# Attention and expert layer on one core: one burst of values for a pair of heads, three banks for transposed probabilities, first keys from ScalarE's queue

## The reference, cut to what matters

```
q = (layernorm(x, g_in) @ Wq) -> 16 heads of 64, * 64**-0.5
k, v = split(layernorm(x, g_in) @ Wkv)              # one head, 64 each
k, v = concat([null_k, k]), concat([null_v, v])     # a null key and value in front
sim = q @ k.T + concat([null_bias, attn_bias])      # 512 x 513 for each head
sim = where(causal or masked, -max, sim)
out = softmax(sim) @ v                              # heads side by side: 512 x 1024
x = x + layernorm(out @ Wo, g_out)
x = x + moe(x)
```

## Time and profile before

| what | value |
|---|---|
| runs | 1820.24, 1817.81, 1814.46 us; median 1817.81 |
| the profiled execution | 1821.24 us, span 1819.5 us |
| TensorE matmul busy | 1644.0 us, 90% of the span |
| TensorE weight load busy | 1369.8 us, 75% |
| VectorE busy | 982.2 us, 54% |
| ScalarE busy | 712.3 us, 39% |
| GpSimd busy | 735.4 us, 40% |
| mean granted TensorE clock | 0.959 of 2.4 GHz |

### The profile page before, as it was taken

One profiled execution on the slowest core, in us unless ns is written; L12 is line 12 of the kernel. 1 busy time (PEld: TensorE's weight loads), 2 busy tenths in 40 slices (PEclk: granted clock), 3 DMA queues, 4 the chain that ended last, 5 costly groups with the idle time before them and its releaser, 6 DMA issues. The chain is left out here.

```text
span 1819.5 us, 36436 instructions
## 1 busy us (share of the span) xinstructions
PE 1644.0 (90%) x10388; PEld 1369.8 (75%) x10389; DVE 982.2 (54%) x2454; ACT 712.3 (39%) x1819; POOL 735.4 (40%) x1204
## 2 busy tenths in 40 slices
PE   6899986999999999996888998869999999879998
PEld 4677766887888888885777776758778788668886
DVE  5434535776777776775544554634334344355555
ACT  3222325776777676772222121103333333311221
POOL 1000234676676676673545551132222222143223
PEclk9989997999999999997999997979999999889999
DMA  6565657776676676766343342043466533244423
GB/s 217 197 209 201 226 205 214 205 219 194 186 221 199 190 224 186 209 181 191 115 136 129 128 151 91 0 174 104 173 225 228 181 104 105 91 145 130 142 92 116
DMA packets 172582, 301.79 MB, mean 166 GB/s; under 512 B 16691, under 2 KB 64355, under 8 KB 170421
## 3 DMA queue, kind: packets, MB, share of 16 engines
q1 hardware_dynamic: 142324, 235.21, 40.2%
q0 software_dynamic: 11280, 35.99, 6.8%
q10 hardware_dynamic: 18864, 29.38, 4.7%
HBM read 187.26 MB, written 113.26 MB: 165 GB/s over the span
## 5 line engine op out<-in xcount | busy, mean ns | idle before, releaser
L737 POOL TENSOR_SCALAR probs<-probs,rsums 128x512 f32<-128x512 f32 (+3 forms) x512 | 265.1, 536 | 199.3 <-DVE rsums L773 199.2
L765 DVE CUSTOM_DVE_ANT_0 scores<-psum,resident 128x514 f32<-128x514 f32 (+3 forms) x512 | 242.8, 484 | 155.3 <-PE psum L880 135.5
L838 ACT ACTIVATE probs<-scores,lowest 128x514 f32<-128x514 f32 (+3 forms) x512 | 284.2, 558 | 33.4 <-DVE lowest L765 32.2
L892 PE MATMUL psum<-ident,probs 128*128 128x128 f32 x1280 | 234.0, 282 | 20.2 <-DVE probsT L780 13.5
L880 PE MATMUL psum<-keys,queries 128*128 (+4 forms) x640 | 221.2, 354 | 22.7 <-DMA queries_and_ones<-q_hi_d 17.4
L892 PEld LDWEIGHTS psum<-ident,probs 128*128 128x128 f32 x1280 | 151.0, 141 | 54.4 <-issue 39.3
L880 PE MATMUL psum<-keys_lo_and_mask,queries_and_ones 128*128 (+4 forms) x640 | 184.5, 297 | 0.0
L912 PE MATMUL psum<-probsT,v_now 128*64 128x128 f32 x2560 | 168.0, 278 | 0.9 <-DVE probsT L780 0.9
L880 PEld LDWEIGHTS psum<-keys,queries 128*128 128x128 f32 x640 | 126.7, 198 | 33.7 <-issue 20.6
L912 PEld LDWEIGHTS psum<-probsT,v_now 128*64 128x64 f32 x2560 | 137.1, 136 | 14.5 <-issue 1.6
L847 ACT ACTIVATE probsT<-psum 128x512 f32<-128x512 f32 (+2 forms) x192 | 93.6, 488 | 134.8 <-PE psum L892 118.3
(11 more groups left out here) (240 smaller groups left out, 3726.4 us busy)
## 6 DMA issues: line engine op xcount, KB each, us to landing
ys_d<-y_out ACTq DMA_DIRECT2D x72, 256.0 KB, 2.0
q_hi_d<-q_hi SPq DMA_DIRECT2D x64, 256.0 KB, 2.7
q_lo_d<-q_lo SPq DMA_DIRECT2D x64, 256.0 KB, 3.0
queries<-q_hi_d SPq DMA_DIRECT2D x64, 256.0 KB, 3.7
queries<-q_lo_d SPq DMA_DIRECT2D x64, 256.0 KB, 4.1
queries_and_ones<-q_hi_d SPq DMA_DIRECT2D x64, 256.0 KB, 4.5
oT_d<-o_out SPq DMA_DIRECT2D x64, 256.0 KB, 2.3
o_in<-oT_d SPq DMA_DIRECT2D x32, 512.0 KB, 4.0
```

The source lines that it names most:

```text
L737: pool.tensor_scalar(out=row, in0=row, scalar1=rsums[:, n % RING:n % RING + 1], scalar2=1.0, op0=ALU.mult, op1=ALU.mult).then_inc(probs_sc ...
L765: dve.tensor_tensor_reduce(out=scores[n % 4][:, 0:CK[i]], in0=score_psum(n), in1=bias_of(resident, i, h), scale=1.0, scalar=3.0e38, op0=AL ...
L838: act.activation(probs[n % RING][:, 0:CK[i]], scores[n % 4][:, 0:CK[i]], ACT.Exp, bias=lowest[:, n % 4:n % 4 + 1], scale=-1.0, accum_out=s ...
L892: last = pe.transpose(probsT_bank[g % 2][:, at + j * P:at + (j + 1) * P], probs[n % RING][:, AHEAD + j * P:AHEAD + (j + 1) * P], ident[:])
```

## The change

The burst covers a whole pair and runs at step 2 of the next pair, once instead of twice; `probsT` holds a whole pair in each of its two tiles, 20 blocks instead of 10. Transposed probabilities get three banks (4, 5, 6), so that a group waits for the group three before it, which the other engine copies. The output gets one bank (7), so that a burst waits for the `add_null` of the pair before. VectorE does `add_null` at step 4, behind the copy of unit 4, instead of at step 3. Score and probability tiles are as long as the units that use them. At the start the three key loads, the mask's and those of the null value column are issued by ScalarE; SyncE issues the two of the null key and then the first queries. Later keys are still loaded by SyncE.

```diff
-        probs = [sb(f"probs{i}", [P, AHEAD + S]) for i in range(RING)]
-        probsT = [sb(f"probsT{i}", [P, 10 * P]) for i in range(2)]
+        probs = [sb(f"probs{i}", [P, CK[ORDER[i % (2 * TB) // 2]]]) for i in range(RING)]
+        probsT = [sb(f"probsT{i}", [P, 20 * P]) for i in range(2)]
...
-        GROUPS = [(0, 1, 0), (1, 1, 4 * P), (2, 2, 8 * P), (4, 1, 0), (5, 1, 3 * P), (6, 2, 6 * P)]
-        NG = len(GROUPS)
+        GROUPS = [(0, 1, 0), (1, 1, 4 * P), (2, 2, 8 * P), (4, 1, 10 * P), (5, 1, 13 * P), (6, 2, 16 * P)]
+        NG, NB = len(GROUPS), 3
...
-        probsT_bank = [bank(psum, 4), bank(psum, 5)]
-        o_bank = [bank(psum, 6), bank(psum, 7)]
+        probsT_bank = [bank(psum, 4 + k) for k in range(NB)]
+        o_bank = bank(psum, 4 + NB)
...
 (SyncE, start)
-            for part in (slice(0, DH), slice(DH, P)):
-                for row, dst in ((0, null_key), (1, null_col)):
-                    sp.dma_start(dst[part, :], ...).then_inc(null_loaded, 16)
-            sp.wait_ge(keys_cleared, 3)
-            load_keys(0)
+            load_null(sp, null_key, 0, null_loaded)
             load_queries(0, 0)
...
 (ScalarE, start)
+            load_keys(act, 0)
+            act.wait_ge(keys_cleared, 3)
+            load_mask(act, 0)
+            load_null(act, null_col, 1, null_col_loaded)
             for n in range(LEAD - 2):
                 exponential(0, n)
...
 (GpSimd, values of the next element)
-                            pool.wait_ge(bursts_weighed, GB * b)
+                            pool.wait_ge(pairs_weighed, NH * b)
...
 (VectorE and ScalarE, copy_probs)
-                if not (isinstance(b, int) and b == 0 and n < 2 * QUAD):
-                    dve.wait_ge(bursts_weighed, GB * b + n // QUAD - 1)
+                if not (isinstance(b, int) and b == 0 and n < 2 * UH):
+                    dve.wait_ge(pairs_weighed, NH * b + n // UH - 1)
...
 (VectorE, body)
-                    if n % UH == 3:
+                    if n % UH == 4:
                         if n > UH:
                             add_null(b, n // UH - 1)
...
 (TensorE, transpose_probs)
-                if n % UH == GROUPS[g % NG][0] and not (isinstance(b, int) and b == 0 and g < 2):
-                    pe.wait_ge(probsT_odd if g % 2 else probsT_even, HG * b + g // 2)
+                if n % UH == GROUPS[g % NG][0] and not (isinstance(b, int) and b == 0 and g < NB):
+                    pe.wait_ge(probsT_even if g % 2 else probsT_odd, HG * b + (g - NB) // 2 + 1)
...
 (TensorE, weigh_values)
+            def weigh_values(b, hp):
+                pe.wait_ge(probsT_even, HG * b + NG // 2 * (hp + 1))
+                pe.wait_ge(probsT_odd, HG * b + NG // 2 * (hp + 1))
+                if hp == 0:
+                    pe.wait_ge(v_ready, b + 1)
+                if not (isinstance(b, int) and b == 0 and hp < 1):
+                    pe.wait_ge(o_ready, NH * b + hp)
+                for n in range(0, UH, 2):
...
 (TensorE, body)
-                    if n % QUAD == 1:
-                        g = n // QUAD - 1
-                        if g >= 0:
-                            weigh_values(b, g)
+                    if n % UH == 2:
+                        hp = n // UH - 1
+                        if hp >= 0:
+                            weigh_values(b, hp)
                         elif not first:
-                            weigh_values(b - 1, GB - 1)
+                            weigh_values(b - 1, NH - 1)
```

More of the change, by code:

```diff
@@ L546, in stage_attend @@
         keys1 = sb("keys_lo_and_mask", [P, 2, AHEAD + S], F32R)
-        scores = [sb(f"scores{i}", [P, AHEAD + S]) for i in range(4)]
+        scores = [sb(f"scores{i}", [P, max(CK[ORDER[0]], CK[ORDER[2]]) if i < 2 else max(CK[ORDER[1]], CK[ORDER[3]])])
+                  for i in range(4)]
         null_key = sb("null_key", [P, 1])
         lowest = sb("lowest", [P, 4])
-        probs = [sb(f"probs{i}", [P, AHEAD + S]) for i in range(RING)]
-        probsT = [sb(f"probsT{i}", [P, 10 * P]) for i in range(2)]
+        probs = [sb(f"probs{i}", [P, CK[ORDER[i % (2 * TB) // 2]]]) for i in range(RING)]
+        probsT = [sb(f"probsT{i}", [P, 20 * P]) for i in range(2)]
         sums, rsums = sb("sums", [P, RING]), sb("rsums", [P, RING])
@@ L578, in stage_attend @@
         QB = UB // QUAD
-        GB = 2 * NH
         WC = DC + MC
@@ L632, in copy_group, with load_keys, load_mask, load_null @@
             width = units * (tile_of(n) + 1) * P
-            return probsT[n % UH // QUAD][:, at:at + width], probsT_bank[group_of(n) % 2][:, 0:width]
+            return probsT[n // UH % 2][:, at:at + width], probsT_bank[group_of(n) % NB][:, 0:width]
+        def load_keys(eng, b):
+            for dst, name in ((keys[0:DH], "k_hi"), (keys[DH:P], "k_hi"), (keys1[0:DH], "k_lo")):
+                eng.dma_start(dst[:, bass.ds(b % 2, 1), AHEAD:AHEAD + S].rearrange("p a s -> p (a s)").bitcast(F32),
+                              dram[name][bass.ds(b, 1)].rearrange("a p s -> p (a s)")).then_inc(keys_loaded, 16)
+        def load_mask(eng, b):
+            eng.dma_start(keys1[DH:DH + 1, bass.ds(b % 2, 1), AHEAD:AHEAD + S].rearrange("p a s -> p (a s)").bitcast(F32),
+                          dram["mask"][:, bass.ds(b * S, S)]).then_inc(keys_loaded, 16)
+        def load_null(eng, dst, row, loaded):
+            for part in (slice(0, DH), slice(DH, P)):
+                eng.dma_start(dst[part, :], cond[row:row + 1, :].rearrange("a d -> d a"),
+                              allow_slow_non_contiguous=True).then_inc(loaded, 16)
         block = ctx.enter_context(nc.Block())
@@ L643, in load_queries @@
                         "a (h d) s -> d (a h) s", d=DH)).then_inc(queries_loaded[hp % 2], 16)
[L645 to L651, removed]
             def load_weights(e, k):
@@ L682, in body @@
                             if hp + 2 == NH:
-                                load_keys(b + 1)
+                                load_keys(sp, b + 1)
+                                load_mask(sp, b + 1)
                             load_queries(b + 1, hp + 2 - NH)
@@ L823, in _ @@
             invert_sums(0, 0)
+            dve.wait_ge(null_col_loaded, 32)
             body(0, first=True)
@@ L843, in copy_probs @@
                 act.wait_ge(probsT_full, UB * b + n + 1)
-                if not (isinstance(b, int) and b == 0 and n < 2 * QUAD):
-                    act.wait_ge(bursts_weighed, GB * b + n // QUAD - 1)
+                if not (isinstance(b, int) and b == 0 and n < 2 * UH):
+                    act.wait_ge(pairs_weighed, NH * b + n // UH - 1)
                 dst, src = copy_group(n)
@@ L911, in weigh_values @@
                             at = column_of(n + head) + j * P
-                            last = pe.matmul(o_bank[hp % 2][head * DH:(head + 1) * DH, cols], v_now[:, j * DH:(j + 1) * DH],
-                                             probsT[half][:, at:at + P], start=(j == 0), stop=(j == i))
-                last.then_inc(bursts_weighed, 1)
+                            last = pe.matmul(o_bank[head * DH:(head + 1) * DH, cols], v_now[:, j * DH:(j + 1) * DH],
+                                             probsT[hp % 2][:, at:at + P], start=(j == 0), stop=(j == i))
+                last.then_inc(pairs_weighed, 1)
             def body(b, first=False, last=False):
```

26 lines of the change are left out of this document (8 added, 18 removed).

## The result

The changed kernel takes 1848.31 us (median of 4 runs, 1842.15 to 1851.55); the kernel before 1819.03 us beside it (4 runs, 1814.46 to 1823.0). The ratio is 1.0155 with a 95% interval of 1.0129 to 1.0181: slower by about 1.6%, clear of the noise. The forecast was 1851 us, range 1825 to 1873.

A forecast was written before the change was run, and what follows sets the result against it. TensorE plus one detour over VectorE bounds a pair; with one burst VectorE's late work delays TensorE. Pairs +19.5, edges +17, start -3.8 sum to +32.7 on 1821.24: 1854, less 3.4 for the median, 1851 us; range 1825 to 1873.

The forecast's parts named there:

- bias 21: VectorE's add for score unit 21, first after the burst; VectorE was to idle over 2 us before it.
- S25: TensorE's scores of unit 25, needing two score banks; said to wait 0.87 us, then take 0.50.
- bias 23: VectorE's add for score unit 23, freeing banks for S25; said to end 5.76 us from the burst's start.
- VectorE's chain: VectorE behind the burst: bias 21 0.48, reciprocal and copy 0.53, null add 0.66, bias 22 and 23 0.69.
- T16+S26: TensorE's transposes of unit 16, then scores of unit 26, behind S25; put at 0.74 us.
- 7.50 for TensorE alone: Pair time if only TensorE bound: 8.03 less 0.38 bank stall less 0.15 for one burst entry and exit.
- Queries: Next element's first query loads, on SyncE behind the output store, come later: +0.6 x 7 = +4 us.
- Values: GpSimd's copy of the next element's values waits for the later, longer burst: +0.7 x 7 = +5 us.
- Loop-backs: At five loop-backs VectorE's stop falls before bias 25 and holds TensorE: 4.4 against 2.8, +1.6 x 5 = +8 us.
- Rival A: Whole pair: TensorE is freed, VectorE keeps up, a pair takes 7.50; 1782 us, chance 0.10.
- C: Pairs slow as forecast, but batch edges cost what they cost before; 1834 us, chance 0.25.
- E: Something else late in each pair, most likely query loads: +0.5 a pair more, 1880 us, chance 0.10.

The follow-up runs named there:

- Keys early: Changed kernel with SyncE issuing the next element's keys and mask one pair earlier, behind that pair's queries: 1823.4 us, ratio 1.0026.

## Why the prediction was right

**The pair.** The mechanism was right in each step: VectorE idle over 2 us in front of bias 21, TensorE held at S25 by bias 23, no wait for transposed probabilities. Its sum was 8.34, measured 8.16. By its own terms, from the rows at 453.46 to 461.62: burst 2.34 (said 2.50), to S21's last matmul 0.34 (0.34), to VectorE's start 0.56 (0.56), VectorE's chain 2.37 (2.36), to TensorE 0.13 (0.14), S25 0.58 (0.50), T16+S26 0.62 (0.74), T17+S27 0.63 (0.65), T18+S28 and the wait 0.59 (0.55). Two terms were mis-sized most. A burst of 40 is not twice the step of a burst of 20: 1.25 held part of the entry and exit. The prediction has this saving, 0.15 us, in its 7.50 for TensorE alone, but left it out of the 8.34. And T16's step of 0.74 was that of a transpose behind four matmuls without a wait; behind a stall it takes 0.62. So +0.32 x 61 = 19.5 became (8.15 - 8.02) x 61 = +8 us.

**The edges.** Said +17, measured 42.6 - 18.9 = +24, within the bounds of the sum, but each of its three parts lies outside its own. Queries: said +4 with bounds 0 and +12, measured about +18 (22.9 us now in the seven intervals just before an element's end, 4.9 before). The step that failed is the price of a later SyncE: it was put at 0.6 us an edge, the rest hidden in S25's wait. The rows give 2.2 us, 7.3 to 7.4 instead of 9.6 from the store to TensorE's turn, of which S25's 0.66 can hide a third at most; and in five of six cases the clock fell behind the wait, which the sum had at nothing. The queue itself was not slower than before. Keys early gave 21 us back, which shows the place; the split between delay and clock is worked out from rows, not measured apart. Values: said +5 with bounds 0 and +8, measured +9 (1.0 to 1.1 each, one 2.7 at the low clock), the chain 2.59 us to the copy (503.32 less 500.73) and 6.56 us to T7 (507.29) against 2.75 and 6.74 plus handover. Loop-backs: said +8 with bounds 0 and +16, measured -4 (9.7 against 14.0 us). The stop on VectorE before bias 25 did hold S28 as said, but only 1.3 to 1.8 us, not 3.6. VectorE's stop was 2.08 us at 424.95 and 1.7 to 1.9 at the other four, instead of 3.0 to 3.7 before; why it is shorter here stays open. In the version with add_null at step 3 the same place loses 3.6 to 4.2, so the slack of the slower pair may have taken part of it. That the three errors left a sum near the forecast is luck.

**The start.** Said -3.8 with a range of -4.5 to -1, measured -2.6 to -2.8. Issue time went as said (3.7 us earlier), and 1.1 us of it came back as a longer way from that issue to the first matmul, with keys and queries under way together. The rule that the prediction takes from the Trainium skill ("Trainium Kernel Development and Optimization", Key Constraints) names both halves: issue time is saved, and the DMA engines are shared. The 3.7 us agree with the first; that the 1.1 us come from the second is not shown.

**Rival A** failed where it was said to: bias 23 ended at 5.61, not before 5.0. With add_null moved it ended at 4.95 and the pair took 7.59, which is A's 7.50 nearly. The rule of the Trainium skill on repeated gaps ("Perfetto Trace Analysis", Optimization Strategy) that A leant on was right about the third bank in the two-burst order (0.4 us a pair) and did not decide in the changed one (0.17). C and E did not happen: edges did cost more, and outside them the longest wait for queries was 0.15 us. That the total fell 2.7 us from the forecast is partly luck, 11 us too much in pairs against 7 too little at edges.

## What to carry to other kernels

Before merging two bursts on the busy engine, count what its partner can do while it runs and what it must do behind it, with the banks between them as the only buffer; an average of 28% idle did not say it here. Move the partner's work into the burst's shadow first: one instruction of 0.66 us was worth 0.56 us a pair. And price the edges of a loop by themselves: 24 of the 32 us that 61 pairs lost here, and nearly all of the 20 to 33 us gained by writing the loop out (between medians, in three orders of the work), lay outside the steady pair. A queue position that has slack in one order can be late in another: the same issues in the same queue cost 5 us at the edges before the change and 23 behind it.

## What the hardware showed that was not expected

- At the jump of a looped body VectorE and ScalarE stood 1.7 to 3.7 us each; with 64 units written out per engine and element, without jump, neither stood over 0.4 us without a named cause in 8 elements. Instruction count fell from 36379 to 34053 in the changed kernel.
- SyncE's issues from the store to the last query load (keys, mask and queries between them), with looped indices, took 5.4 us at five edges and 5.9 at the first looped one; with constants 4.1 to 4.2.
- Forty matmuls of a burst step by 2.34 us, not by twice 1.25.
- A wait of 2.6 to 3.1 us on TensorE left the following matmuls at the lower clock in five of the six looped cases (granted clock 0.50, 0.58 us where the others take 0.38); behind the sixth, of 2.63 us, it stayed at 1.00.
